# State-space projections straight from the transposed input, and the first unit's C replicas ahead of its transposes

## The chip, the cores and the metric

The kernel runs on one core of a Trainium2 chip, in fp32. The metric is the device time of one execution in microseconds; of several executions the median is given. Engines are called by name: TensorE (PE), VectorE (DVE), ScalarE (ACT), GpSimd (POOL) and SyncE (SP), whose queue issues the DMAs.

## The reference

Sixteen sequences of 512 tokens of width 128 pass attention, a mixture of eight experts, a state-space layer solved as a fixed point, and the mixture again, each with a layer norm ahead of it and a residual sum behind it. The change touches the state-space layer:

```python
xz = hidden_states @ W_in.T
x, z = (xz[..., :D_INNER], xz[..., D_INNER:])          # D_INNER = 256
x_dbl = x @ W_x.T
dt_low = x_dbl[..., :DT_RANK]                          # DT_RANK = 8
B0 = x_dbl[..., DT_RANK:DT_RANK + D_STATE]             # D_STATE = 16
C0 = x_dbl[..., DT_RANK + D_STATE:]
delta = jax.nn.softplus(dt_low @ W_dt.T + b_dt)
def fp_step(y_prev):
    x_tilde = (x - y_prev) @ W_mix.T + y_prev
    bc = _shift1(y_prev) @ W_bc.T
    Bt = bc_normalize(B0 + bc[..., :D_STATE])
    Ct = bc_normalize(C0 + bc[..., D_STATE:])
    y = _selective_scan(x_tilde, delta, A, Bt, Ct, D)  # h = exp(delta A) h + delta u B; y = sum_n h C + D u
    return layer_norm(y)
y0 = jnp.zeros_like(x)
y_star = jax.lax.fori_loop(0, 8, lambda i, y: y + STEP * (fp_step(y) - y), y0)
y = fp_step(y_star)
```

Here `hidden_states` is the layer norm of the residual; its transpose is `xnT` in the kernel. As y starts at zero, the first step needs only what comes from x.

## The kernel before, in words

A loop of 16 turns (one a sequence) runs attention, `mixture`, `ssm_inputs`, `first_unit`, an inner loop of 8 turns with two `scan_unit` each (one for each half of 256 tokens), a last `scan_unit`, `ssm_output` and `mixture`. Each engine has its own program, written out by hand in order; semaphores (the `Signal` objects) tie them together. Weights stay on the chip. The next sequence's attention start is done inside the last mixture.

`ssm_inputs` turns the normed tokens on TensorE (L444), ScalarE copies them to `xnT` (L909), then TensorE makes x transposed (`xT`, L618, 256 channels as two blocks of 128, each 512 tokens), ScalarE copies each block (L1003), TensorE makes the 8 low-rank rows (L623), ScalarE copies them to `dtlow` (L1006), whose ninth row is ones so that the bias `b_dt` rides in `w_dt`, and TensorE makes delta's argument (L628) into PSUM banks 5 and 6. B and C (L633, bank 7) and the mixed x (L639, banks 0 and 1) come from `xT` too, two matmuls for each of four token blocks, one for each block of channels.

The softplus is max(v, 0) + ln(1 + e) with e = exp(-|v|), with a correction of the rounding of 1 + e by a slope 1 - e/2. ScalarE makes Abs (L1010), Exp (L1013) and Ln (L1015); VectorE makes the max (L1439), 1 + e (L1442), the slope (L1444) and four more steps up to delta (L1459). Then ScalarE squares B and C and takes the root, VectorE multiplies x and delta (`du`, L1462) and normalises B and C into `bcn` (L1487). ACT_TABLE_LOAD rows are loads of ScalarE's function tables, which the compiler places.

A unit has 16 scans (p = 0 to 15). A scan covers a pair of channel blocks of 32 for one group m of four states. It needs da, the exponential of delta times the decay, from a replica of delta on the four state rows (`repeat_delta`, L657, block cb of eight, into banks 5, 6, 7, 4 by turns; ScalarE's exponentials, L1035, two a scan, signal `da_ready`), and its input (`scan_input`, L803, from `scan_in`, which L1470 on VectorE fills for m = 0 to 2 and L1069 on ScalarE for m = 3). In the first unit the scans follow `FIRST`: j = 0 and 1 for all four m, then the pairs j = 2, 3 for m = 2, 0, 1, 3. As both halves' da are needed, all 32 exponentials are made here. VectorE scans (L1508), and a memset at the first token of every second row (`da_cut`) cuts the state between the two rows of a scan; GpSimd multiplies each state by C (L1669), for which `crep` holds C's replicas (`first_c`, L696, bank 3, in two halves, copied at L1042), and `first_sum` adds up products on TensorE (L708) into bank 3. Scans from the fifth on wait for the product four places back and for a small DMA that keeps the last state. From p = 3 on, input p waits for scan p - 3, since three banks hold the inputs.

At the end TensorE makes the C replicas of the second half (`front_c`, L757), ScalarE fills the first inputs of the next unit (L1069 at L1157) and copies the replicas (L1159), and TensorE does the last `first_sum`. Then the loop begins with input 0 and VectorE's scans (L1569).

The order of TensorE in the first unit is: replicas 0 to 3 of delta; input 0; first half of C; input 1; replicas 4 and 5; input 2; second half of C; inputs 3 to 5; replicas 6 and 7; then inputs with sums between.

## Time and profile before

| | us |
|---|---|
| Time, median of 3 runs | 10725.11 |
| Lowest and highest of them | 10701.15, 10734.08 |
| Profiled execution, time | 10721.71 |
| Profiled execution, span | 10719.8 |
| Mean granted TensorE clock, share of full | 0.96 |

The profile is of one execution. Its page gives busy times, slices and groups of instructions for the whole span. Since every sequence runs through all stages, the timeline of one sequence (instructions in order of time, neighbours of one kind merged into one row with a count) is what shows where an engine waits; in its rows the brackets give the idle time of that engine before the row and what ended it. The clock of a stretch stands in the table of windows: 1.00 is 2.4 GHz and 0.50 is 1.2 GHz.

### The profile page before, as it was taken

The page shows a single profiled execution, that of the slowest core. Times are in us where ns is not written, and L with a number is a line of the kernel's source. Part 1 is how long each engine was busy: PE and PEld are TensorE (multiplying, and loading weights), DVE is VectorE, ACT ScalarE, POOL GpSimd, SP SyncE. Part 2 cuts the span into 40 slices and gives each one's busy share as a digit, 9 for nine tenths or more (in the row PEclk, how much of TensorE's full clock was granted, in tenths as well). Part 3 has the DMA queues.
Part 4 walks back from the last instruction along what each step waited for, and adds up shares of the span by engine and source line. Part 5 has one row for each costly group of instructions (what it writes and reads, how often), then busy time and mean ns, then how long its engine had stood idle before and what let it go on. Part 6 is the DMA issues. An engine that isn't in the chain of part 4 may idle for free.

```text
span 10719.8 us, 254606 instructions
## 1 busy us (share of the span) xinstructions
PE 9419.7 (88%) x86284; PEld 6248.4 (58%) x86284; DVE 9037.8 (84%) x16766; ACT 7334.3 (68%) x15096; POOL 6110.9 (57%) x4900
## 2 busy tenths in 40 slices
PE   7988889888898888988889888898888988889888
PEld 4656656566565665656656566565665656656566
DVE  6978879789797887978879788797887979879698
ACT  5866758677576776757768576675766857668576
POOL 1936719367293672926729277292762927639276
PEclk9999999999999999999999999999999999999999
DMA  0000000000000000000000000000000000000000
GB/s 21 0 3 1 1 3 0 3 1 1 3 0 3 1 2 3 0 3 1 2 3 0 3 1 1 3 0 3 1 1 3 0 3 1 2 2 0 3 1 3
DMA packets 648318, 23.40 MB, mean 2 GB/s; under 512 B 629169, under 2 KB 646978, under 8 KB 647362
## 3 DMA queue, kind: packets, MB, share of 16 engines
q1 hardware_dynamic: 647746, 16.11, 3.6%
q8 instruction: 318, 5.21, 0.2%
q14 instruction: 254, 2.08, 0.1%
HBM read 9.40 MB, written 4.19 MB: 1 GB/s over the span
## 4 chain that ended last, share of the span: by engine, by line
DVE 31%; PE 25%; issue 19%; POOL 17%; ACT 5%; DVEq 2%; DMA 1%; POOLq 1%; SPq 0%; ACTq 0%
POOL work L1669 16%; DVE work L1569 15%; DVE work L1559 6%; PE ps L573 4%; PE ps L578 4%; PE ps L588 3%; PE ps L521 3%; PE ps L509 2%; ACT da L947 1%; DMA hend<-work 1%; PE ps L486 1%; DVE scan_in L1470 1%; DVE stats L1187 1%; DVEq L1553 1%; PE ps L803 1%
## 5 line engine op out<-in xcount | busy, mean ns | idle before, releaser
L1669 POOL TENSOR_TENSOR work<-work,crep 128x512 f32<-128x512 f32 x4608 | 5768.7, 1278 | 4530.9 <-ACT crep L1042 3948.6
L1069 ACT ACTIVATE scan_in<-du,bcn 128x256 f32<-128x256 f32 x8832 | 3685.6, 497 | 36.9 <-PE ps L803 26.5
L1569 DVE TENSOR_TENSOR_SCAN work<-da,hend,ps 128x256 f32<-128x256 f32 x4608 | 3037.0, 724 | 31.8 <-PE ps L803 29.9
L803 PE MATMUL ps<-w_ident,scan_in 128*128 128x128 f32 x18432 | 2713.2, 282 | 278.7 <-ACT scan_in L1069 103.0
L803 PEld LDWEIGHTS ps<-w_ident,scan_in 128*128 128x128 f32 x18432 | 2032.1, 143 | 1232.8 <-issue 713.7
L1559 DVE TENSOR_TENSOR_SCAN work<-da,ps 128x512 f32<-128x512 f32 x2048 | 2363.4, 1200 | 17.0 <-PE ps L803 0.5
L793 PE MATMUL ps<-work,w_sel 128*32 128x256 f32 x17792 | 1406.2, 392 | 158.4 <-POOL work L1669 146.8
L981 ACT ACTIVATE work<-ps,w_gate_b 128x512 f32<-128x512 f32 x512 | 352.0, 687 | 895.6 <-PE ps L573 892.8
L1294 DVE TENSOR_REDUCE smax<-ps 128x1 f32<-128x512 f32 x1024 | 661.0, 686 | 202.0 <-PE ps L486 198.0
L793 PEld LDWEIGHTS ps<-work,w_sel 128*32 128x32 f32 x17792 | 355.4, 108 | 619.3 <-POOL work L1669 364.0
L947 ACT ACTIVATE da<-ps 128x512 f32<-128x512 f32 x1024 | 573.4, 596 | 164.5 <-PE ps L509 157.2
L1395 DVE SCALAR_TENSOR_TENSOR work<-ps,w_up_b,work 128x512 f32<-128x512 f32 x512 | 377.8, 749 | 272.5 <-PE ps L578 231.2
L573 PE MATMUL ps<-xnT,gate_w 128*128 128x512 f32 x1024 | 568.8, 639 | 0.0
L578 PE MATMUL ps<-xnT,up_w 128*128 128x512 f32 x1024 | 551.1, 621 | 0.0
L588 PEld LDWEIGHTS ps<-down_w,work 128*128 128x128 f32 x4096 | 489.9, 192 | 88.2 <-issue 68.9
L757 PE MATMUL ps<-w_ident,bcn 128*32 128x128 f32 x17408 | 531.0, 274 | 0.0
L1085 ACT ACTIVATE yscT<-ps 128x512 f32<-128x512 f32 x288 | 172.0, 597 | 496.0 <-PE ps L793 496.0
L588 PE MATMUL ps<-down_w,work 128*128 128x128 f32 x4096 | 501.0, 276 | 4.0 <-DVE work L1395 4.0
L1053 ACT ACTIVATE u_sb<-ps 128x512 f32<-128x512 f32 x256 | 153.3, 599 | 501.9 <-DVE du L1524 501.9
L742 PE MATMUL ps<-mix_y,yT 128*128 128x256 f32 x2048 | 489.5, 382 | 0.0
L757 PEld LDWEIGHTS ps<-w_ident,bcn 128*32 128x32 f32 x17408 | 460.0, 110 | 45.7 <-issue 43.0
L509 PE MATMUL ps<-da 98*128 98x512 bf16 x1024 | 394.9, 390 | 103.9 <-ACT da L947 59.1
(196 smaller groups left out, 12415.6 us busy)
## 6 DMA issues: line engine op xcount, KB each, us to landing
hend<-work SPq DMA_DIRECT2D x2304, 1.0 KB, 1.8
x_in<-in_x SPq DMA_DIRECT2D x17, 256.0 KB, 2.8
out<-work SPq DMA_DIRECT2D x16, 256.0 KB
gate_w<-in_gate_w SPq DMA_DIRECT2D x1, 1024.0 KB, 4.9
up_w<-in_up_w SPq DMA_DIRECT2D x1, 1024.0 KB, 7.0
down_w<-in_down_w SPq DMA_DIRECT2D x1, 1024.0 KB, 9.0
w_w_in<-in_w_in SPq DMA_DIRECT2D x1, 256.0 KB
w_w_zy<-in_w_zy SPq DMA_DIRECT2D x1, 256.0 KB
```

What stands on the lines that cost most here:

```text
L573: mm = eng.matmul(bank(u % 2), gate_w[:, e, f * P:(f + 1) * P], xnT[:], start=True, stop=True)
L578: mm = eng.matmul(bank(2 + u % 2), up_w[:, e, f * P:(f + 1) * P], xnT[:], start=True, stop=True)
L588: mm = eng.matmul(blocks(6 + e % 2)[:, tb, :], hid[:, e % 2, f, tb * P:(tb + 1) * P], down_w[:, e, f, :], start=(tb == 0 and f == 0), stop ...
L757: mm = eng.matmul(ps[GC * k:GC * (k + 1), 6 + m // 2, c:c + P], bcn[:, hf, tb, 1, n:n + 1].broadcast_to([P, GC]), ident[:], start=(m % 2 = ...
L793: mm = eng.matmul(ps[GC * q:GC * (q + 1), 3, j % 2 * TH:(j % 2 + 1) * TH], w["sel"][:], prod[:, p % PROD, q % 2 * TH:(q % 2 + 1) * TH], st ...
L803: mm = eng.transpose(ps[:, bank, c:c + P], scan_in[:, m, tb, 2 * j + s].rearrange("p k c -> p (k c)"), ident[:])
L947: eng.activation(probsT[:, h % HG, kb, :], bank(3 + (TB * h + kb) % 2), ACT.Exp, scale=SCALE).then_inc(exped.sem, exped.up(at))
L1069: ins = eng.activation(scan_in[:, m, tb, :, k, :], du[:, hf, tb, :].rearrange("p (e c) -> p e c", c=GC), ACT.Copy, scale=bcn[:, hf, tb, 0, ...
L1294: eng.tensor_reduce(smax[:, h % 2, qb:qb + 1], bank(u % 3), AX, ALU.max).then_inc(maxed.sem, maxed.up(at))
L1559: eng.tensor_tensor_scan(hst[:, p % NHID, :], da[:, 0, 2 * p:2 * p + 2, :].rearrange("p s t -> p (s t)"), bank(RING[p % 4]), 0.0, ALU.mult ...
L1569: ins = eng.tensor_tensor_scan(hst[:, p % NHID, half], da[:, 1, 2 * p + s, :], ps[:, RING[p % 4], half], hend[:, 2 * p + s:2 * p + s + 1], ...
L1669: eng.tensor_tensor(prod[:, to, :].rearrange("p (s t) -> p s t", s=2), hst[:, p % NHID, :].rearrange("p (s t) -> p s t", s=2), crep[:, hf, ...
```

## The change

Once a launch, ahead of the loop, TensorE multiplies weights with weights: the x half of `W_in` with `W_mix` (`x_mix`), with the B and C rows of `W_x` (`x_bcw`), and with the low-rank rows and then `W_dt` (`x_dt`); ScalarE copies the results out of PSUM. The factors are loaded into `work`, which is free then; `W_in`'s x half is loaded untransposed (`w_in_c`), its z half as `w_in_z`. `cT`, which lay in `dtlow`, gets a tensor of its own.

In `ssm_inputs` delta's argument, B, C and the mixed x are each made by one matmul per token block from `xnT`. `xT`, `dtlow` and their copies are gone. The bias enters by four matmuls with a contraction of one row, issued ahead of the wait for `xnT`. ScalarE does a one-column Exp between its Sqrt and the copy of `xnT`; the slope of the softplus moves from VectorE to ScalarE (Identity, signal `dl_slope`); the copy of x_mixed goes ahead of the copy of B and C and the root.

In the first unit all of C's replicas are made at once (`repeat_c`, into banks 2 and 3) between delta's replicas 1 and 2, and ScalarE copies them with one instruction ahead of its exponentials. Input 2 waits for that copy, as its bank is 2. Delta's replicas 4, 5, 6 and 7 come singly, behind inputs 3, 4, 7 and 8. VectorE's cut comes ahead of every second scan and waits for the exponentials of two scans; before, the first two cuts covered four scans each.

```diff
+FIRST_REP_AT = (3, 4, 7, 8)
...
-            "w_in": [P, 2 * DI], "w_x": [P, DB, DR + 2 * NS], "a_log": [P, NG],
-            "w_bc": [P, DB, 2 * NS], "w_zy": [P, DB, DI], "w_mix": [P, DB, DI],
+            "w_in_z": [P, DI], "a_log": [P, NG],
+            "w_bc": [P, DB, 2 * NS], "w_zy": [P, DB, DI],
...
-        w_dt = sb("w_dt", [DR + 1, DI])
+        b_dt = sb("b_dt", [1, DI])
+        x_mix = sb("x_mix", [P, DI])
+        x_bcw = sb("x_bcw", [P, 2 * NS])
+        x_dt = sb("x_dt", [P, DI])
...
+        early = {"w_mix": work[:, 0:512].rearrange("p (h d) -> p h d", h=DB),
+                 "w_x": work[:, 512:592].rearrange("p (h d) -> p h d", h=DB),
+                 "w_in_c": work[:, 592:848].rearrange("p (h d) -> p h d", h=DB),
+                 "w_dt": work[0:DR, 1024:1280]}
+        low_in = work[0:DR, 848:976]
...
             def ssm_inputs(at):
...
+                for tb in range(TB):
+                    eng.matmul(wide[:, tb, :], one[0:1, 0:1].broadcast_to([1, P]), b_dt[:],
+                               start=(tb % 2 == 0), stop=False)
                 eng.wait_ge(n_ssm.xnT.sem, n_ssm.xnT.count(at, 1))
-                for h in range(DB):
-                    mm = eng.matmul(bank(5 + h), w["w_in"][:, h * P:(h + 1) * P], xnT[:],
-                                    start=True, stop=True)
-                    mm.then_inc(xT_done.sem, xT_done.up(at))
-                for h in range(DB):
-                    eng.wait_ge(xT_copied.sem, xT_copied.count(at, h + 1))
-                    mm = eng.matmul(ps[0:DR, 4, :], w["w_x"][:, h, 0:DR], xT[:, h, :],
-                                    start=(h == 0), stop=(h == DB - 1))
-                mm.then_inc(dt_done.sem, dt_done.up(at))
-                eng.wait_ge(dt_copied.sem, dt_copied.count(at, 1))
                 for tb in range(TB):
-                    mm = eng.matmul(wide[:, tb, :], dtlow[:, tb * P:(tb + 1) * P], w_dt[:],
-                                    start=(tb % 2 == 0), stop=(tb % 2 == 1))
+                    mm = eng.matmul(wide[:, tb, :], xnT[:, tb * P:(tb + 1) * P], x_dt[:],
+                                    start=False, stop=(tb % 2 == 1))
                 mm.then_inc(dl_done.sem, dl_done.up(at))
                 for tb in range(TB):
-                    for h in range(DB):
-                        mm = eng.matmul(ps[:, 7, tb * 32:(tb + 1) * 32], xT[:, h, tb * P:(tb + 1) * P],
-                                        w["w_x"][:, h, DR:DR + 2 * NS], start=(tb == 0 and h == 0),
-                                        stop=(tb == TB - 1 and h == DB - 1))
+                    mm = eng.matmul(ps[:, 7, tb * 32:(tb + 1) * 32], xnT[:, tb * P:(tb + 1) * P],
+                                    x_bcw[:], start=(tb == 0), stop=(tb == TB - 1))
                 mm.then_inc(bc_done.sem, bc_done.up(at))
                 for tb in range(TB):
-                    for h in range(DB):
-                        mm = eng.matmul(ps[:, tb // HB, (tb % HB) * DI:(tb % HB + 1) * DI],
-                                        xT[:, h, tb * P:(tb + 1) * P], w["w_mix"][:, h, :],
-                                        start=(tb % HB == 0 and h == 0),
-                                        stop=(tb % HB == HB - 1 and h == DB - 1))
+                    mm = eng.matmul(ps[:, tb // HB, (tb % HB) * DI:(tb % HB + 1) * DI],
+                                    xnT[:, tb * P:(tb + 1) * P], x_mix[:],
+                                    start=(tb % HB == 0), stop=(tb % HB == HB - 1))
                 mm.then_inc(xmix_done.sem, xmix_done.up(at))
 
                 eng.wait_ge(x_mixed_a.sem, x_mixed_a.count(at, 1))
                 eng.wait_ge(dl_ready.sem, dl_ready.count(at, 1))
-                for cb in range(4):
-                    if cb == 2:
-                        eng.wait_ge(bc_normed.sem, bc_normed.count(at, 1))
+                for cb in range(2):
+                    repeat_delta(at, cb)
+                eng.wait_ge(bc_normed.sem, bc_normed.count(at, 1))
+                repeat_c(at, 0, 2)
+                for cb in range(2, 4):
                     repeat_delta(at, cb)
                 first_unit(at)
...
                         eng.wait_ge(scanned.sem, scanned.count(at, p - 2))
+                    elif p == 2:
+                        eng.wait_ge(c_copied.sem, c_copied.count(at, 1))
                     scan_input(at, m, j, FIRST_BANK[p])
-                    if p in (0, 2):
-                        first_c(at, p // 2)
-                    if p in (1, 5):
-                        j = 2 + p // 5
-                        eng.wait_ge(da_ready.sem, da_ready.count(at, NM * (j - 1)))
-                        repeat_delta(at, 2 * j)
-                        repeat_delta(at, 2 * j + 1)
+                    if p in FIRST_REP_AT:
+                        cb = NK + FIRST_REP_AT.index(p)
+                        eng.wait_ge(da_ready.sem, da_ready.count(at, NM * (cb // 2 - 1)))
+                        repeat_delta(at, cb)
                     if p in FIRST_SUM_AT:
                         first_sum(at, FIRST_SUM_AT.index(p))
                 front_c(at, 1, 1)
                 first_sum(at, 4)
...
+                repeat_c(at, hf, 6)
+
+            def repeat_c(at, hf, bank):
...
                             mm = eng.matmul(
-                                ps[GC * k:GC * (k + 1), 6 + m // 2, c:c + P],
+                                ps[GC * k:GC * (k + 1), bank + m // 2, c:c + P],
...
+            for h in range(DB):
+                eng.matmul(ps[:, 0, 0:DI], early["w_in_c"][:, h, :], early["w_mix"][:, h, :],
+                           start=(h == 0), stop=(h == DB - 1))
+            for h in range(DB):
+                eng.matmul(ps[:, 1, 0:2 * NS], early["w_in_c"][:, h, :], early["w_x"][:, h, DR:DR + 2 * NS],
+                           start=(h == 0), stop=(h == DB - 1))
+            for h in range(DB):
+                mm = eng.matmul(ps[0:DR, 2, 0:P], early["w_x"][:, h, 0:DR], early["w_in_c"][:, h, :],
+                                start=(h == 0), stop=(h == DB - 1))
+            mm.then_inc(folded, 1)
+            eng.wait_ge(fold_kept, 1)
+            eng.matmul(ps[:, 3, 0:DI], low_in, early["w_dt"], start=True, stop=True).then_inc(folded, 1)
+            eng.wait_ge(fold_kept, 2)
             begin_with(start, len(PE_START))
             with eng.Fori(0, B) as b:
...
             def ssm_inputs(at):
                 root(at, n_ssm)
+                eng.activation(exp_one[:], one[:], ACT.Exp)
                 copy_turned(at, n_ssm, xnT[:], bank(4))
-                for h in range(DB):
-                    eng.wait_ge(xT_done.sem, xT_done.count(at, h + 1))
-                    eng.activation(xT[:, h, :], bank(5 + h), ACT.Copy
-                        ).then_inc(xT_copied.sem, xT_copied.up(at))
-                eng.wait_ge(dt_done.sem, dt_done.count(at, 1))
-                eng.activation(dtlow[0:DR, :], ps[0:DR, 4, :], ACT.Copy
-                    ).then_inc(dt_copied.sem, dt_copied.up(at))
                 eng.wait_ge(dl_done.sem, dl_done.count(at, 1))
...
                 eng.wait_ge(dl_exp.sem, dl_exp.count(at, 1))
+                eng.activation(delta[:].rearrange("p b c -> p (b c)"), sp[1], ACT.Identity, bias=one[:], scale=-0.5
+                               ).then_inc(dl_slope.sem, dl_slope.up(at))
                 eng.activation(sp[3], sp[1], ACT.Ln, bias=one[:]).then_inc(dl_ln.sem, dl_ln.up(at))
                 eng.wait_ge(bc_done.sem, bc_done.count(at, 1))
                 eng.activation(bcq[:].rearrange("p b k n -> p (b k n)"), ps[:, 7, 0:TB * 2 * NS],
                                ACT.Square).then_inc(sq_done.sem, sq_done.up(at))
-                eng.activation(x_bc[:].rearrange("p b c -> p (b c)"), ps[:, 7, 0:P], ACT.Copy)
-                eng.wait_ge(ss_done.sem, ss_done.count(at, 1))
-                eng.activation(nrm[:], ss[:], ACT.Sqrt).then_inc(nrm_done.sem, nrm_done.up(at))
                 eng.wait_ge(xmix_done.sem, xmix_done.count(at, 1))
                 eng.activation(x_mixed[:].rearrange("p b c -> p (b c)"),
                                ps[:, 0:2, :].rearrange("p k c -> p (k c)"), ACT.Copy
                                ).then_inc(x_mixed_a.sem, x_mixed_a.up(at))
+                eng.activation(x_bc[:].rearrange("p b c -> p (b c)"), ps[:, 7, 0:P], ACT.Copy)
+                eng.wait_ge(ss_done.sem, ss_done.count(at, 1))
+                eng.activation(nrm[:], ss[:], ACT.Sqrt).then_inc(nrm_done.sem, nrm_done.up(at))
                 eng.activation(exp_one[:], one[:], ACT.Exp)
                 eng.wait_ge(du_done.sem, du_done.count(at, 1))
                 eng.wait_ge(bc_normed.sem, bc_normed.count(at, 1))
                 fill(at, 0, NM - 1, 0)
                 fill(at, 0, NM - 1, 1).then_inc(filled_a.sem, filled_a.up(at))
+                eng.wait_ge(c_rep.sem, c_rep.count(at, 1))
+                eng.activation(crep[:, 0].rearrange("p m t -> p (m t)"),
+                               ps[:, 2:4, :].rearrange("p k c -> p (k c)"), ACT.Copy
+                               ).then_inc(c_copied.sem, c_copied.up(at))
                 for p, (m, j) in enumerate(FIRST):
                     for cb in (2 * j, 2 * j + 1):
                         eng.wait_ge(dl_rep.sem, dl_rep.count(at, cb + 1))
@@ -1036,12 +1034,6 @@
                             "p (f t) -> p f t", f=2), ACT.Exp,
                                              scale=decay[:, g:g + 1])
                     ins.then_inc(da_ready.sem, da_ready.up(at))
...
+            eng.wait_ge(folded, 1)
+            eng.activation(x_mix[:], ps[:, 0, 0:DI], ACT.Copy)
+            eng.activation(x_bcw[:], ps[:, 1, 0:2 * NS], ACT.Copy)
+            eng.activation(low_in, ps[0:DR, 2, 0:P], ACT.Copy).then_inc(fold_kept, 1)
+            eng.wait_ge(folded, 2)
+            eng.activation(x_dt[:], ps[:, 3, 0:DI], ACT.Copy).then_inc(fold_kept, 1)
...
-                eng.tensor_scalar(sp[2], sp[1], 1.0, None, ALU.add)
+                eng.tensor_scalar(sp[2], sp[1], 1.0, None, ALU.add).then_inc(vchain.sem, vchain.up(at))
                 flat = delta[:].rearrange("p b c -> p (b c)")
-                eng.tensor_scalar(flat, sp[1], -0.5, 1.0, ALU.mult, ALU.add
-                                  ).then_inc(vchain.sem, vchain.up(at))
                 eng.wait_ge(vchain.sem, vchain.last(at))
                 eng.scalar_tensor_tensor(out=sp[2], in0=sp[2], scalar=-1.0, in1=sp[1],
                                          op0=ALU.add, op1=ALU.subtract
                                              ).then_inc(vchain.sem, vchain.up(at))
                 eng.wait_ge(vchain.sem, vchain.last(at))
+                eng.wait_ge(dl_slope.sem, dl_slope.count(at, 1))
                 eng.tensor_tensor(sp[2], sp[2], flat, ALU.mult).then_inc(vchain.sem, vchain.up(at))
...
-                    if p in (0, 4):
-                        eng.wait_ge(da_ready.sem, da_ready.count(at, p + 4))
-                        eng.memset(da[:, 0, g + 1::NCB, 0], 0.0).then_inc(da_cut.sem, da_cut.up(at))
-                        eng.wait_ge(da_cut.sem, da_cut.last(at))
-                    if p >= 8 and p % 2 == 0:
+                    if p % 2 == 0:
                         eng.wait_ge(da_ready.sem, da_ready.count(at, p + 2))
-                        eng.memset(da[:, 0, g + 1:g + 4:2, 0], 0.0).then_inc(da_cut.sem, da_cut.up(at))
+                        step = NCB if p < NP // 2 else 2
+                        eng.memset(da[:, 0, g + 1:g + step + 2:step, 0], 0.0).then_inc(da_cut.sem, da_cut.up(at))
                         eng.wait_ge(da_cut.sem, da_cut.last(at))
```

Left out of the diff: the semaphores of removed and added steps, the loads' count, the memset of `dtlow` and the arrays' preparation on the host.

## Rows read from the trace of the kernel before

**Rows 1.** Page, part 1: busy us of each engine (share of span), xinstructions.
```profile
PE 9419.7 (88%) x86284; PEld 6248.4 (58%) x86284; DVE 9037.8 (84%) x16766; ACT 7334.3 (68%) x15096; POOL 6110.9 (57%) x4900
```

**Rows 2.** Timeline of VectorE in the loop: start, length, engine, line, operation.
```profile
248.60 0.18 DVE L1516 TENSOR_REDUCE ss<-bcq 128x4 f32<-128x64 f32 x1
...
295.25 0.19 DVE L1516 TENSOR_REDUCE ss<-bcq 128x4 f32<-128x64 f32 x1
```

**Rows 3.** Timeline, all engines, 177 to 188 us: projections of the first sequence.
```profile
177.33 1.10 PE L444 MATMUL ps<-w_ident,work 128*128 128x128 f32 x4 [3.47 <-DVE work L1205]
...
178.47 0.60 ACT L909 ACTIVATE xnT<-ps 128x512 f32<-128x512 f32 x1 [1.78 <-PE ps L444]
...
179.12 3.62 PE L618 MATMUL ps<-xnT,w_w_in 128*128 128x512 f32 x4 [0.69 <-ACT xnT L909]
...
185.22 1.99 PE L628 MATMUL ps<-w_dt,dtlow 9*128 9x256 f32 x8 [0.68 <-ACT dtlow L1006]
...
187.25 1.02 ACT L1010 ACTIVATE scan_in<-ps 128x1024 f32<-128x1024 f32 x1 [2.08 <-PE ps L628]
```

**Rows 4.** Timeline, 188 to 198 us: softplus of the first sequence.
```profile
188.29 1.28 ACT L1013 ACT_TABLE_LOAD   x1
...
188.31 1.23 DVE L1439 TENSOR_SCALAR scan_in<-ps 128x1024 f32<-128x1024 f32 x1 [9.19 <-ACT scan_in L1010]
...
189.59 1.06 ACT L1013 ACTIVATE scan_in<-scan_in 128x1024 f32<-128x1024 f32 x1
...
191.28 0.69 DVE L1444 TENSOR_SCALAR delta<-scan_in 128x1024 f32<-128x1024 f32 x1
...
196.08 1.22 DVE L1459 TENSOR_TENSOR delta<-scan_in 128x1024 f32<-128x1024 f32 x1
```

**Rows 5.** Timeline, 199 to 215 us: fills, exponentials, replicas, first product.
```profile
199.33 6.90 DVE L1470 TENSOR_TENSOR scan_in<-du,bcn 128x1024 f32<-128x1024 f32 x6
...
199.39 3.31 ACT L1069 ACTIVATE scan_in<-du,bcn 128x256 f32<-128x256 f32 x8 [0.55 <-DVE bcn L1487]
...
202.60 4.69 ACT L1035 ACTIVATE da<-ps,decay 128x512 f32<-128x512 f32 x8
...
207.34 3.64 PE L657 MATMUL ps<-w_ident,delta 128*32 128x128 f32 x64 [2.68 <-ACT da L1035]
...
207.55 2.33 DVE L1508 TENSOR_TENSOR_SCAN work<-da,ps 128x512 f32<-128x512 f32 x2
...
213.68 0.60 ACT L1042 ACTIVATE crep<-ps 128x512 f32<-128x512 f32 x1 [3.58 <-PE ps L696]
...
214.36 19.78 POOL L1669 TENSOR_TENSOR work<-work,crep 128x512 f32<-128x512 f32 x16 [213.91 <-ACT crep L1042]
```

**Rows 6.** Timeline, 221 to 234 us: end of the first unit, loop's first scan.
```profile
221.86 2.33 DVE L1508 TENSOR_TENSOR_SCAN work<-da,ps 128x512 f32<-128x512 f32 x2 [0.29 <-PE ps L803]
...
227.96 3.30 ACT L1069 ACTIVATE scan_in<-du,bcn 128x256 f32<-128x256 f32 x8 [1.66 <-PE ps L803]
...
229.70 1.93 PE L757 MATMUL ps<-w_ident,bcn 128*32 128x128 f32 x64
...
232.30 1.09 PE L803 MATMUL ps<-w_ident,scan_in 128*128 128x128 f32 x8
...
233.25 5.21 DVE L1569 TENSOR_TENSOR_SCAN work<-da,hend,ps 128x256 f32<-128x256 f32 x8 [1.27 <-PE ps L803]
```

**Rows 7.** Windows: length, busy (count) of PE, PEld, DVE, ACT, POOL; clock; DMA; GB/s.
```profile
178.00:180.00 2.00, 1.31 (x3) 0.64 (x3) 0.96 (x2) 0.60 (x1) 0.00 (x0) 0.76 0.00 0
...
180.00:182.00 2.00, 2.00 (x4) 0.67 (x2) 0.00 (x0) 0.60 (x1) 0.00 (x0) 0.50 0.00 0
...
182.00:184.00 2.00, 2.00 (x6) 0.27 (x4) 0.00 (x0) 0.60 (x1) 0.00 (x0) 0.89 0.00 0
...
208.00:210.00 2.00, 2.00 (x44) 1.85 (x40) 1.89 (x2) 2.00 (x4) 0.00 (x0) 0.50 0.00 0
...
228.00:230.00 2.00, 0.76 (x20) 0.59 (x24) 1.77 (x4) 2.00 (x6) 2.00 (x2) 1.00 0.15 1
```

51 lines of the change are left out of this document (14 added, 37 removed).

## The prediction, made before the change was run

> **What bounds the kernel now.** I read the page's busy times first. TensorE is busy 88% of the span and VectorE 84% [rows 1], but such a share is a mean over stages, so it prices nothing. The order of time comes next. In the fixed-point loop the first `ss` reduction of two neighbouring turns stands at 248.60 and 295.25 us [rows 2], so a turn takes 46.65 us, and in the whole launch there are 16 sequences of 8 turns. The change leaves the turns alone. It works on the stretch ahead of them: from the normalised transposes of the state-space input (177.33) to the first scan of the loop (233.25) [rows 3, 6]. That stretch is a chain with waits and little overlap, so time taken off it should come off every sequence. It runs 16 times; in the tenth and the sixteenth sequence it is as long within 0.2 us, in the fifth 1.3 us shorter.
>
> I cut the stretch at three moments: *a*, the start of the Abs on ScalarE, 187.25 [rows 3]; *D*, the end of the last addition into delta, 196.08 + 1.22 = 197.30 [rows 4]; and *L*, the first scan of the loop, 233.25 [rows 6]. So D is a + 10.05 and L is D + 35.95.
>
> **Part 1: projections, transposes to a.** Removed: the 128x512 matmuls of L618 (3.62 us), two ScalarE copies of xT, the L623 matmuls, and the dtlow copy between them and L628 [rows 3]; every hop was PE to ACT and back. Added: four one-row bias matmuls (each of this kernel's fp32 matmuls has two records, so 8 records of 256 columns), issued behind the transposes and ahead of the wait for xnT; then 8 records of the same width from xnT. The nearest rows are the 8 records of L628, 1.99 us at full clock, 0.25 each [rows 3]; its contraction has 9 rows, no row shows one of 1, and I take the same price, since L618 and L628 share columns and not rows and both follow the columns. At half clock I take 0.43 a record (L618: 3.62/4 = 0.91 for twice the columns, mostly at half clock). The clock matters: TensorE sits idle 3.47 us before these transposes, its clock is 0.76 of full in 178 to 180, 0.50 in 180 to 182 and 0.89 in 182 to 184 [rows 3, 7], which puts the low stretch at about 179.1 to 182.5. I assume that it stays there. The transposes end at 178.43. To 179.1 some 2.8 bias records pass; the other 5.2 cost 2.24, to 181.35. To 182.5 pass 2.7 of the xnT records, the other 5.3 at 0.23 end at 183.7. So a = 183.75, 3.5 us earlier. If the clock stays low for all of them: 178.43 + 0.7 + 13.2 x 0.43 = 184.8, or 185.2 with drains, and the gain is 2.05. If the bias rows cost less, a is near 183.4 and the gain 3.85.
>
> The xnT copy (178.47 to 179.07) must not be late. Ahead of it ScalarE now does a table load and the one-column Exp. It idles 1.78 us before that copy, from 176.69 [rows 3]; 1.28 for the load [rows 4] and 0.2 fit, and even 1 us of lateness would be covered by the bias matmuls, which run to 181.35. I cost it at nothing; without both covers it would be 1.5.
>
> **Part 2: softplus, a to D.** Now Abs (1.02), table load 188.29 (1.28), Exp (1.06), and then VectorE until D [rows 3, 4]. The load goes away, because the table came earlier: 1.28 us. No row shows Abs or Identity right behind an Exp; Abs runs here behind a Sqrt table and the loop's Identity runs behind one too. The Trainium skill (ScalarE: Activation LUTs, "Table sets: the hidden batching unit") says copy, identity and abs are in every set; no run here shows it for these two. The same page ("What ACT_TABLE_LOAD costs") prices a switch at 1.28 for the load and 1.38 more for a drain; this trace shows the load 0.02 us behind the Abs [rows 3, 4] and nothing like a drain, and by the page the sum below would gain 1.38 x 16 = 22 us more. The slope (L1444, 0.69 long, next instruction 0.72 later by the rows) [rows 4] moves to ScalarE, an Identity of 1.06 like the Exp, which finishes under the 1.23 us of the two-operand step. VectorE starts the add about 0.6 earlier relative to the rest. Against it: the max L1439 (1.23) lay under the table load and now ends at a + 2.29, 0.19 after the Exp [rows 4]. So D = a + 10.05 - 1.28 - 0.6 + 0.19 = a + 8.35, gain 1.7; Ln, still 1.28 load and 1.15 long but behind the Identity, ends at a + 5.65, ahead of the final addition (a + 7.1). Square, x_mixed (1.01), x_bc, Sqrt load and nrm now end at a + 8.8, and VectorE asks for nrm after du, at about D + 1.3 = a + 9.6: hidden by 0.8. x_mixed needs its matmuls, now 8 records instead of 16 and ending by a + 4.5 even at half clock, against a + 5.95. Bounds of this part: 1.4 (each hop 0.1 worse) to 1.9 (the max hidden).
> Together D moves from 197.30 to 192.1, gain 5.2, between 3.45 and 5.75.
>
> **Part 3: first unit, D to L.** Today VectorE starts the first scan at D + 10.25, only when four exponential pairs are there (eight records from 202.60, 0.586 each); TensorE issues half of the C replicas behind the second pair of delta replicas, ScalarE copies them at 213.68 after a 3.58 us wait, and GpSimd starts at 214.36 = D + 17.06, running 16 products in 19.78 [rows 5]. Since a scan from the fifth on waits for a product, this start paces all.
> New order on TensorE: delta replicas 0 and 1, wait for bcn (D + 2.0), all C replicas (64 records, 1.93 us as in L757 [rows 6]), replicas 2 and 3. TensorE has by then been idle for 5 us (mix ends near 186.5), and idling 3.47 us was enough for a low clock soon after [rows 3, 7], so I charge half clock to the first pair: 3.64, as L657 at 207.34 [rows 5] against the 1.93 of L757 for as many records at full clock [rows 6]. It ends at D + 3.75, C at 5.7. ScalarE's own fill ends at D + 5.4 [rows 5], then the C copy of 1.02 to D + 6.8. The wait placed ahead of the exponentials costs them 202.60 -> D + 5.3 against D + 6.8: 1.5 us later, repaid because two copies and the 3.58 wait are gone. First pair of exponentials 9.1; VectorE's fills end at 8.93 [rows 5]; first scan D + 9.3 (now only two pairs awaited, each pair of scans behind one memset). GpSimd starts at D + 10.5, 6.6 earlier. TensorE's new wait for the C copy before input 2 holds back inputs 2 to 15, and is over at D + 6.8; input 2 also needs VectorE's fill at 8.93, so it costs nothing.
> Then VectorE at 2.58 a pair (2.33 for the two scans at 221.86, 0.25 for memset and waits) [rows 6]: fifth scan over at 15.65. Input 7 waits for it: 16.35, replica 6 17.3, input 8 18.0, replica 7 18.95 (0.66 an input, half of 1.93 a replica). ScalarE has done nine pairs at 17.35, waits for replica 7, and ends pair 10 at 19.55; six more at 1.17 end at 26.6. VectorE wants that pair at 19.6, so the stall hardly touches it. Input 15 at 27.25, ScalarE's fill of the next unit 3.30 [rows 6], 30.6; loop input to first scan 0.95 [rows 6]; L = D + 31.6. GpSimd's 14th product, for which the last partial sum waits and which holds L now, is done at 28.5. Gain 35.95 - 31.6 = 4.35. GpSimd is free for the loop at D + 33.7 against 39.25, so it doesn't take the place. Bounds: 1.9 if a second low stretch covers inputs 3 to 8 (about 2.4: two replicas and two inputs at half speed and one replica more), 5.0 if none occurs and replica 7 comes earlier.
>
> **Once per launch.** One more weight load, six matmuls, three copies, a matmul and a copy stand ahead of the first normalisation. I estimate some 16 records, most of half the width of L618's or less, at 3.0 in all from that line's price, and the load and the chained copies at 1.5 from L909's 0.60 a copy of 512 columns [rows 3]: 4.5 us, between 3 and 7. Nothing covers it.
>
> **Sum.** 16 x (5.2 + 4.35) = 153; less 4.5, and less 4 for a sequence or two in which the low clock falls worse: 144. The profiled execution took 10721.71, 1.9 over its span and 3.4 under the median 10725.11. 10721.7 - 144 + 3.4 = 10581 us.
>
> **Rivals.** (1) *The clock takes back the second gain.* With fewer matmuls and over 5 us of idleness, TensorE is at half clock from D until replica 7. C replicas end at D + 7.6, the copy at 8.65, first scan 11.2, replica 7 23.4, L = D + 36.5, gain -0.5; with a at 185.2 also, 3.2 a sequence, 51 in all: 10678. For it: 208 to 210 are at 0.50 today although TensorE is busy throughout [rows 7]. Against: the low stretch seen in 178 to 184 was over by 182.5, with TensorE at work [rows 7]. The Trainium skill (TensorE: Matmul & The Clock Gate, Part 1) says that the throttled state is the default and activity releases it, which speaks against removing matmuls; by that rule the time is this rival's. Chance 0.12.
> (2) *Table loads stay.* If Abs or Identity doesn't live in the Exp table, one or two loads of 1.28 return: 16 x 2.56 = 41, 10622. Chance 0.06.
> (3) *Slower.* Half clock lasts to the loop. Then inputs (1.12) and partial sums (1.28) pace the end too: input 15 at D + 35, C of the next unit 3.9, last sum 41.5, L = D + 43, 7 later than now against a first gain of 3.75: 3.3 lost, 53 + 4.5, 10782. It decides for slower from where the low stretch outlasts about input 12. Against it: in 228 to 230 TensorE works 0.76 us of 2 and is at full clock [rows 7]. Chance 0.05.
> (4) *More*, under 10545: bias rows cheap and no second low stretch. Chance 0.07. The forecast itself 0.70.
>
> **How the numbers follow.** The bounds of the parts give 16 x (3.45 + 1.9) - 7 = 79 to 16 x (5.75 + 5.0) - 3 = 169, so 10646 to 10556 by the median; rival 2 lies inside, and 10 us below is room for the terms that I rounded. Range 10545 to 10645, which leaves out rivals 1, 3 and 4, about 0.22. About 0.3% (32 us) is what a measurement can tell from no change. Faster by more: 0.91; within: 0.04, the tails of rivals 1 and 3; slower: 0.05.
>
> **What would show it.** Right: Abs starting 5.3 us after the xnT copy instead of 8.8, no table load between Abs and Exp, delta done 8.35 after Abs; one 1.02 us C copy before the exponentials; GpSimd's first product some 10.5 us after D, first scan of the loop 31.6 after. Wrong: the clock at 0.50 in several 2 us stretches behind D, replica 7 holding ScalarE longer than 2 us, or a loop turn other than 46.65, which would make all of this small beside 128 times the difference.

## The result and the profile after

The changed kernel took 10604.16 us (median of 4 runs, 10599.98 to 10630.49) against 10721.96 for the kernel before on the same chip: a ratio of 0.9897, with a 95% interval of 0.988 to 0.9914, so some 110 us less by the ratio (92 to 129), 118 by the two medians. The same kernel timed twice more beside the experiments gave 0.9885 (0.9868 to 0.9901) and 0.9916 (0.9903 to 0.993). The forecast was 10581 in a range of 10545 to 10645. Its profiled execution took 10630.49 (span 10628.6), 91 under that of the kernel before, and was the slowest of its four.

Page of the changed kernel, part 1: busy us of each engine (share of span), xinstructions.

```profile
PE 9367.1 (88%) x86042; PEld 6259.7 (59%) x86042; DVE 9021.3 (85%) x16781; ACT 7321.0 (69%) x15068; POOL 6111.1 (57%) x4900
```

Beside [rows 1] nothing moves by more than 0.6%. The stretch that the change works on has to be read in the order of time. Timeline of the changed kernel, first sequence, from the turned norm to the end of delta: start, length, engine, line, operation, records, and in brackets the idle time ahead and what ended it.

```profile
181.65 1.10 PE L450 MATMUL ps<-w_ident,work 128*128 128x128 f32 x4 [3.47 <-DVE work L1203]
...
182.68 3.15 PE L623 MATMUL ps<-b_dt,one 1*128 1x256 f32 x8
182.78 0.60 ACT L907 ACTIVATE xnT<-ps 128x512 f32<-128x512 f32 x1 [0.27 <-PE ps L450]
...
185.76 3.78 PE L627 MATMUL ps<-x_dt,xnT 128*128 128x256 f32 x8
...
189.58 1.02 ACT L1002 ACTIVATE scan_in<-ps 128x1024 f32<-128x1024 f32 x1 [6.20 <-PE ps L627]
...
190.64 1.06 ACT L1005 ACTIVATE scan_in<-scan_in 128x1024 f32<-128x1024 f32 x1
...
191.73 1.15 ACT L1007 ACTIVATE delta<-scan_in,one 128x1024 f32<-128x1024 f32 x1
...
192.90 1.28 ACT L1009 ACT_TABLE_LOAD   x1
...
194.19 1.15 ACT L1009 ACTIVATE scan_in<-scan_in,one 128x1024 f32<-128x1024 f32 x1
...
196.57 1.22 DVE L1456 TENSOR_TENSOR delta<-scan_in 128x1024 f32<-128x1024 f32 x1
```

The Abs starts 6.80 us after the xnT copy (forecast 5.3, before 8.78 in [rows 3]), and delta is done at 197.79, 8.21 after the Abs (forecast 8.35). No table load stands between Abs, Exp and Identity. The bias records take 3.15 and the xnT records 3.78, where 8 records of this width took 1.99 at full clock in [rows 3]. The windows say why. Windows of the changed kernel: length, busy (count) of PE, PEld, DVE, ACT, POOL, granted clock, DMA share, GB/s.

```profile
182.00:184.00 2.00, 2.00 (x8) 1.40 (x9) 1.27 (x3) 1.10 (x3) 0.00 (x0) 0.84 0.00 0
184.00:186.00 2.00, 2.00 (x6) 1.16 (x5) 0.00 (x0) 0.00 (x0) 0.00 (x0) 0.50 0.00 0
186.00:188.00 2.00, 2.00 (x5) 1.61 (x6) 0.00 (x0) 0.00 (x0) 0.00 (x0) 0.50 0.00 0
188.00:190.00 2.00, 2.00 (x8) 1.67 (x7) 0.00 (x0) 0.42 (x1) 0.00 (x0) 0.50 0.00 0
190.00:192.00 2.00, 2.00 (x13) 1.84 (x13) 1.36 (x2) 1.94 (x3) 0.00 (x0) 0.96 0.00 0
...
200.00:202.00 2.00, 2.00 (x46) 2.00 (x42) 2.00 (x2) 2.00 (x6) 0.00 (x0) 0.50 0.01 4
```

In [rows 7] the low stretch covered about 179.1 to 182.5; here half clock holds for three whole windows, while TensorE is busy throughout, and it holds all but the first two or three of the 16 records (0.84 in 182 to 184 puts its start at about 183.4, 0.96 in 190 to 192 its end at about 190.2). From delta to the loop, same timeline:

```profile
197.93 3.64 PE L654 MATMUL ps<-w_ident,delta 128*32 128x128 f32 x64 [5.41 <-DVE delta L1456]
...
201.32 3.16 PE L742 MATMUL ps<-w_ident,bcn 128*32 128x128 f32 x64
...
204.29 1.93 PE L654 MATMUL ps<-w_ident,delta 128*32 128x128 f32 x64
204.55 1.02 ACT L1026 ACTIVATE crep<-ps 128x1024 f32<-128x1024 f32 x1 [1.46 <-PE ps L742]
...
208.14 2.33 DVE L1502 TENSOR_TENSOR_SCAN work<-da,ps 128x512 f32<-128x512 f32 x2
...
209.61 6.22 POOL L1662 TENSOR_TENSOR work<-work,crep 128x512 f32<-128x512 f32 x5 [209.16 <-DVE work L1502]
...
210.25 1.60 PE L654 MATMUL ps<-w_ident,delta 128*32 128x128 f32 x32 [0.17 <-ACT da L1033]
...
212.82 1.66 PE L654 MATMUL ps<-w_ident,delta 128*32 128x128 f32 x32
...
217.02 0.69 ACT L1033 ACTIVATE da<-ps,decay 128x512 f32<-128x512 f32 x1 [1.05 <-PE ps L654]
...
218.62 7.62 ACT L1033 ACTIVATE da<-ps,decay 128x512 f32<-128x512 f32 x13 [0.91 <-PE ps L654]
...
230.54 1.09 PE L788 MATMUL ps<-w_ident,scan_in 128*128 128x128 f32 x8 [0.78 <-ACT scan_in L1061]
...
231.49 5.21 DVE L1563 TENSOR_TENSOR_SCAN work<-da,hend,ps 128x256 f32<-128x256 f32 x8 [1.65 <-POOL work L1662]
...
246.32 0.18 DVE L1510 TENSOR_REDUCE ss<-bcq 128x4 f32<-128x64 f32 x1
...
292.82 0.19 DVE L1510 TENSOR_REDUCE ss<-bcq 128x4 f32<-128x64 f32 x1
```

GpSimd no longer waits for the C copy [rows 5] but for the first scan, and starts 11.8 us after delta instead of 17.06. The C replicas ran mostly at half clock too (3.16). ScalarE waits 1.05 and 0.91 for replicas 6 and 7, and the loop's first scan comes 33.70 after delta. Its bracket names GpSimd, but its input starts 0.95 ahead of it, as in the kernel before (232.30 and 233.25, [rows 6]), and that input waits for ScalarE's fill.

Half clock comes back once more behind delta. Windows of the same execution:

```profile
210.00:212.00 2.00, 1.83 (x34) 1.37 (x34) 1.86 (x4) 2.00 (x5) 2.00 (x2) 0.66 0.15 1
212.00:214.00 2.00, 2.00 (x28) 1.59 (x31) 1.70 (x3) 2.00 (x4) 2.00 (x3) 0.50 0.07 1
```

This second stretch, from about 210.6 to 214.0, falls on replicas 4 and 5, which take 1.60 and 1.66 instead of 1.08, and on an input. It is there in 13 of the 16 sequences, whose first scan of the loop comes 33.44 to 33.73 after delta. In the other three (the tenth, thirteenth and sixteenth) half clock ends by 3.0 us after delta, the C replicas take 1.94, the second stretch comes only some 27 us after delta, and the loop's first scan comes at 32.36.

The first turn of the loop is 46.50 us here. The median turn is 46.53 in the kernel before and 46.52 in this one, so the 46.65 of [rows 2] was a turn slightly longer than most.

Means over all 16 sequences of each profiled execution, read from the same rows. The first column runs from the start of the xnT copy to the Abs, then to *D*, then to *L*; the fourth is their sum; the last is the timed ratio to the kernel before on the same chip.

| kernel | copy to a | a to D | D to L | copy to L | ratio (95%) |
|---|---|---|---|---|---|
| before | 8.81 | 10.05 | 35.46 | 54.33 | 1 |
| changed | 6.95 | 8.21 | 33.38 | 48.54 | 0.9897 (0.988-0.9914) |
| e1 changed again | 6.89 | 8.21 | 33.23 | 48.33 | 0.9885 (0.9868-0.9901) |
| e2 projections, softplus only | 6.86 | 8.21 | 33.95 | 49.02 | 0.9911 (0.9894-0.9927) |
| e3 first unit only | 8.82 | 10.04 | 32.24 | 51.10 | 0.995 (0.9934-0.9967) |
| e4 without the softplus part | 6.99 | 10.05 | 32.02 | 49.06 | 0.9893 (0.9877-0.991) |
| e5 TensorE busy ahead of D | 6.93 | 8.21 | 33.58 | 48.72 | 0.9929 (0.9912-0.9945) |
| e6 bias rows early | 4.35 | 8.21 | 33.25 | 45.81 | 0.9876 (0.986-0.9893) |
| e7 replicas earlier | 7.06 | 8.21 | 32.69 | 47.96 | 0.9915 (0.9899-0.9932) |
| e8 e5, e6 and e7 | 4.34 | 8.21 | 31.59 | 44.14 | 0.9859 (0.9842-0.9875) |
| e9 changed, on a third chip | 6.99 | 8.21 | 33.29 | 48.49 | 0.9916 (0.9903-0.993) |
| e10 bias on 128 rows | 5.20 | 8.21 | 32.07 | 45.48 | 0.9875 (0.986-0.989) |
| e11 TensorE busy ahead of the transposes | 6.74 | 8.21 | 33.00 | 47.95 | 0.9911 (0.9896-0.9926) |
| e12 e10, early, with e5 and e7 | 4.20 | 8.21 | 31.66 | 44.07 | 0.9861 (0.9846-0.9876) |

The stretch lost 5.79 us a sequence, 93 a launch, less 4.3 for the work ahead of the first sequence: 88 of the 91 us between the two profiled executions. What remains of a sequence beside this stretch lasted 613.1 us before and 612.9 after, but 613.2 and 610.5 in the two further profiles of the changed kernel itself (e1, e9): some 42 us a launch between two executions of one program, outside this stretch. It goes with the clock: in that part of a sequence TensorE is at half clock for 36.3 us in e1 and 33.9 in e9, and over the sequences of all fourteen profiles the length of the part and its time at half clock have a correlation of 0.72. Why the clock differs between two executions no run here explains. The table's stages are therefore the finer instrument, and times are compared by the medians and intervals of one chip alone. Even the ratio of one kernel moves between chips: 0.9885 (e1) and 0.9916 (e9) have intervals that do not meet. The changed kernel was not timed on the chip of e5 to e8, so their ratios are set against a base that is uncertain by 0.3%.

### The profile page after: what moved, and what is told of

Same layout as the page of the kernel before. It is cut to its first block, busy times and chain, and to the rows that moved or that the text cites. A ratio compares the mean times of both kernels' runs of the same rounds, so it can differ in the third digit from the quotient of the medians.

```text
span 10628.6 us, 254158 instructions
## 1 busy us (share of the span) xinstructions
PE 9367.1 (88%) x86042; PEld 6259.7 (59%) x86042; DVE 9021.3 (85%) x16781; ACT 7321.0 (69%) x15068; POOL 6111.1 (57%) x4900
## 3 DMA queue, kind: packets, MB, share of 16 engines
q14 instruction: 254, 2.08, 0.1%
## 4 chain that ended last, share of the span: by engine, by line
DVE 31%; PE 27%; issue 17%; POOL 15%; ACT 5%; DVEq 2%; DMA 1%; POOLq 1%; SPq 0%; ACTq 0%
DVE work L1563 15%; POOL work L1662 15%; DVE work L1553 6%; PE ps L579 4%; PE ps L584 4%; PE ps L594 3%; PE ps L527 2%; PE ps L515 2%; PE ps L788 1%; ACT da L945 1%; DMA hend<-work 1%; PE ps L492 1%; PE ps L654 1%; DVE stats L1185 1%; DVEq L1547 1%
## 5 line engine op out<-in xcount | busy, mean ns | idle before, releaser
L742 PE MATMUL ps<-w_ident,bcn 128*32 128x128 f32 x18432 | 579.8, 279 | 0.0
L742 PEld LDWEIGHTS ps<-w_ident,bcn 128*32 128x32 f32 x18432 | 507.3, 112 | 47.0 <-issue 44.3
```

What stands on the lines that cost most here:

```text
L742: mm = eng.matmul(ps[GC * k:GC * (k + 1), bank + m // 2, c:c + P], bcn[:, hf, tb, 1, n:n + 1].broadcast_to([P, GC]), ident[:], start=(m % ...
```

## The experiments

**e1, the changed kernel again**, as the base for e2, e3 and e4 on their chip.

> The changed kernel once more, for its clock and stage lengths beside the partial kernels. Both theories: 0.989 of before; copy of xnT to the loop's first scan 48.5 us as a mean of the 16 sequences, against 54.3. If the profiled execution of the first result was an unlucky one (it took 10630 where three others took 10600 to 10608), this one should show fewer or shorter stretches at half clock: some 1 us less in the stages a (Abs) and L (first scan of the loop).

It measured 10604.16, and its stages repeat those of the changed kernel within 0.2 us.

**e2, projections and softplus alone**: the changed kernel with the first unit's old order.

```diff
-                for cb in range(2):
-                    repeat_delta(at, cb)
-                eng.wait_ge(bc_normed.sem, bc_normed.count(at, 1))
-                repeat_c(at, 0, 2)
-                for cb in range(2, 4):
+                for cb in range(4):
+                    if cb == 2:
+                        eng.wait_ge(bc_normed.sem, bc_normed.count(at, 1))
                     repeat_delta(at, cb)
...
+                    if p in (0, 2):
+                        first_c(at, p // 2)
```

> Weight products, bias rows, table ahead and slope on ScalarE, but the old order of the first unit (C replicas in two halves behind inputs 0 and 2, delta replicas in pairs). Theory A (each part is worth what its stage shows in the changed kernel): the stages up to D give 1.86 + 1.84 = 3.7 us a sequence, D to L stays 35.5: 16 x 3.7 - 4.3 = 55 us, ratio 0.9949. Theory B (the projections' shortcut takes from the first unit by making TensorE idle, so that its replicas run at half clock): D to L gets longer than 35.5, ratio above 0.997 if by 2 us.

It measured 10627.55, 100 us less than before; D to L is 33.95, 1.5 less than before, though this part of the program is the old one. Timeline of e2, first sequence:

```profile
207.31 1.95 PE L653 MATMUL ps<-w_ident,delta 128*32 128x128 f32 x64 [1.24 <-ACT da L1040]
...
210.93 0.60 ACT L1047 ACTIVATE crep<-ps 128x512 f32<-128x512 f32 x1 [0.87 <-PE ps L692]
...
211.60 18.52 POOL L1678 TENSOR_TENSOR work<-work,crep 128x512 f32<-128x512 f32 x15 [211.15 <-ACT crep L1047]
```

The replicas that took 3.64 in [rows 5] take 1.95, and the wait of 3.58 ahead of the second C copy is 0.87. With delta some 3.8 us sooner after the copy, the low stretch falls on other instructions. The gain of this part is larger than the stages up to delta say.

**e3, first unit alone**: the kernel before with the new order of replicas, one C copy and a memset for each second scan.

```diff
-                for cb in range(4):
-                    if cb == 2:
-                        eng.wait_ge(bc_normed.sem, bc_normed.count(at, 1))
+                for cb in range(2):
+                    repeat_delta(at, cb)
+                eng.wait_ge(bc_normed.sem, bc_normed.count(at, 1))
+                repeat_c(at, 0, 2)
+                for cb in range(2, 4):
                     repeat_delta(at, cb)
...
-                    if p in (0, 2):
-                        first_c(at, p // 2)
```

> The kernel before with only the new order of the first unit. Theory A: D to L falls from 35.5 to 33.4, 2.1 x 16 = 33 us, ratio 0.997. Theory B: with the old projections TensorE is warm at D, C replicas take 1.93 instead of 3.2 and the first pair of delta replicas 1.93 instead of 3.6; D to L falls to 32 or less, 3.5 x 16 = 56 us, ratio 0.995.

It measured 10669.39, 58 us less. Timeline and a window of e3, first sequence:

```profile
196.84 1.96 PE L659 MATMUL ps<-w_ident,delta 128*32 128x128 f32 x64 [3.10 <-ACT x_mixed L1013]
198.74 1.95 PE L747 MATMUL ps<-w_ident,bcn 128*32 128x128 f32 x64
```

```profile
198.00:200.00 2.00, 2.00 (x79) 1.78 (x72) 1.90 (x6) 1.44 (x6) 0.00 (x0) 1.00 0.05 12
```

Behind the old projections the same replicas run at full clock, and D to L is 32.24, 1.1 shorter than in the changed kernel. The two halves alone give 100 and 58 us, together 123 (e1). By the stages, copy to L, they give 5.31 and 3.23 a sequence and together 6.00, not 8.54. The parts don't add.

**e4, without the softplus part**: no early Exp, slope back on VectorE.

```diff
-                eng.activation(exp_one[:], one[:], ACT.Exp)
...
-                eng.activation(delta[:].rearrange("p b c -> p (b c)"), sp[1], ACT.Identity, bias=one[:], scale=-0.5
-                               ).then_inc(dl_slope.sem, dl_slope.up(at))
...
+                eng.tensor_scalar(flat, sp[1], -0.5, 1.0, ALU.mult, ALU.add
+                                  ).then_inc(vchain.sem, vchain.up(at))
```

> The changed kernel without the early Exp table and with the slope back on VectorE. If this part is worth what its stage shows, a to D returns from 8.21 to 10.05 and the time is 1.84 x 16 = 29 us over the changed kernel, ratio 0.992. Rival: the gain is hidden, because a later step (root, fills, C copy) ends last anyway: then it stays at 0.989.

It measured 10611.86, 8 us over e1 and not 29; 8 us is within the intervals of the two. The stage a to D is 1.84 longer, as it should be, but D to L is 1.21 shorter, so copy to L is 0.73 longer, some 12 us a launch. TensorE's first C replicas take 2.14 us instead of 3.16: coming 1.84 us later to D, they meet less of the low stretch. And in none of the 16 sequences does half clock come back before the loop. The step's own size was right, its worth was not.

**e5, TensorE kept busy until D.** Five idle matmuls behind the projections write into bank 3, which the C replicas overwrite before anything reads it.

```diff
                 mm.then_inc(xmix_done.sem, xmix_done.up(at))
+                for _ in range(5):
+                    eng.matmul(bank(3), ident[:], xnT[:], start=True, stop=True)
```

> The changed kernel with five idle 512-column matmuls (into PSUM bank 3, read by nobody) behind the mixed-x matmuls, so that TensorE works through the wait for delta; nothing that is used is changed. Clock theory: delta replicas 0 and 1 and the C replicas fall from 3.64 and 3.16 to about 1.93 each, D to L from 33.3 to about 32, as in the kernel with only the new order (32.24): 1.2 x 16 = 19 us less than the changed kernel, ratio 0.987. Rival: the replicas aren't what D to L hangs on (fills and exponentials are): 0.9885 as the changed kernel, D to L at 33.3.

The first replicas take 1.96, the C replicas 1.95, and the first scan comes 9.00 after D instead of 10.02 in the mean; yet the time is not better (10631.98, 0.9929), and D to L is 33.58 in the mean. In all 16 sequences half clock came back twice before the loop, some 9 and 26 us after D, and in 8 of them each of the two stretches was twice as long as in the others. Windows and timeline of e5, third sequence:

```profile
1528.00:1530.00 2.00, 2.00 (x33) 1.55 (x33) 1.87 (x4) 2.00 (x4) 2.00 (x2) 0.50 0.15 1
...
1546.00:1548.00 2.00, 2.00 (x26) 1.17 (x29) 1.77 (x4) 1.56 (x4) 0.98 (x2) 0.50 0.18 9
```

```profile
1552.06 1.38 DVE L1565 TENSOR_TENSOR_SCAN work<-da,hend,ps 128x256 f32<-128x256 f32 x2 [3.30 <-PE ps L790]
```

The second stretch falls on the last inputs, the partial sums and the next C replicas, and VectorE waits 3.30 us for the loop's first input. Those 8 sequences have a D to L of some 34.9, the others some 32.3. The low stretch was moved, not removed: between the copy and L TensorE is at half clock for 17.2 us in the mean, against 16.6 in the changed kernel.

**e6, the bias rows ahead of the transposes**, behind a wait for the addition that last reads their banks.

```diff
-                turn_norm(at, n_ssm, blocks(4))
+                eng.wait_ge(summed.sem, summed.count(at, NE - 1))
                 for tb in range(TB):
                     eng.matmul(wide[:, tb, :], one[0:1, 0:1].broadcast_to([1, P]), b_dt[:],
                                start=(tb % 2 == 0), stop=False)
+                turn_norm(at, n_ssm, blocks(4))
```

> The changed kernel with the four bias matmuls ahead of the transposes instead of behind them, in the 3.47 us in which TensorE waits for the normalised tokens. Clock theory: the xnT matmuls find a TensorE that has worked shortly before and take 2 us, so Abs starts 2.7 us after the copy of xnT instead of 6.8: 4.1 us a sequence less, of which a part returns behind D; between 20 and 65 us under the changed kernel, ratio 0.983 to 0.987. Rival (the clock falls all the same): xnT matmuls 3.4 us long, Abs at 4.2, and everything given back behind D: ratio 0.988.

It measured 10579.72, 0.9876; its interval still overlaps e1's. Timeline of e6, first sequence:

```profile
179.19 1.99 PE L623 MATMUL ps<-b_dt,one 1*128 1x256 f32 x8
...
183.86 0.60 ACT L908 ACTIVATE xnT<-ps 128x512 f32<-128x512 f32 x1 [0.26 <-PE ps L450]
...
184.51 3.58 PE L628 MATMUL ps<-x_dt,xnT 128*128 128x256 f32 x8 [0.69 <-ACT xnT L908]
```

At full clock the one-row records cost what the forecast took: 1.99 for eight. The price was right, the clock wasn't. The xnT records behind still meet half clock, so the Abs comes 4.35 after the copy, as the rival said. Its other half, that all of this comes back behind D, is not in the stages: D to L is 33.25, as in e1.

**e7, replicas 4 to 7 earlier**: they ride on inputs 3, 4, 5 and 6, and ScalarE's fill for the next unit waits for 12 inputs instead of 16.

```diff
-FIRST_REP_AT = (3, 4, 7, 8)
+FIRST_REP_AT = (3, 4, 5, 6)
...
-                eng.wait_ge(b_done.sem, b_done.count(at, NP))
+                eng.wait_ge(b_done.sem, b_done.count(at, 12))
```

> The changed kernel with delta replicas 6 and 7 behind inputs 5 and 6 instead of 7 and 8, and with ScalarE's fill of the next unit's first inputs waiting for 12 inputs of this unit instead of 16. If ScalarE's wait for replicas 6 and 7 (1.05 + 0.91 us) and its 0.81 us wait for input 15 set the loop's first scan: 1.7 to 2.5 us less from D to L, 27 to 40 us, ratio 0.985. Rival: GpSimd's products end last, first scan only 0.7 us earlier, 11 us, ratio 0.9875.

D to L is 32.69, 0.6 less, as the rival had it; as a time (10620.53, 0.9915) that is inconclusive.

**e8, e5, e6 and e7 together.**

> The edits of the three kernels beside it together. If they add up: copy of xnT to the loop's first scan 48.4 - 4.1 - 1.2 - 2 = 41 us, 117 us under the changed kernel, ratio 0.9775. If the half clock gives part back again, as it did between the parts of the change: ratio 0.981 to 0.985.

It measured 10561.09, 0.9859, less of a gain than either expectation: copy to L is 44.14, 4.4 less than in the changed kernel and not 7.3. The edits of e5 and e7, of little worth alone, bring 1.7 beside e6. Here low stretches did go away: between the copy and L TensorE is at half clock for 6.9 us in the mean instead of 16.6, and in 8 of 16 sequences it has full clock from D to L. What remains of a sequence is longest here, 613.7.

**e9, the changed kernel in the third group.**

> The changed kernel as the base for the three kernels beside it, on their chip: ratio 0.9885 again, Abs 6.9 us after the copy of xnT, clock at half from about 183 to 190 us in the first sequence.

It measured 10606.13, with the stages of e1, but a ratio of 0.9916 and not 0.9885.

**e10, the bias on 128 rows.** The bias is loaded on all partitions and multiplied by the identity: the same 8 records of 256 columns in the same place, with 128 rows of contraction instead of one. The stationary operand changes with the rows, from one element read 128 times to the identity.

```diff
-        b_dt = sb("b_dt", [1, DI])
+        b_dt = sb("b_dt", [P, DI])
...
-                    eng.matmul(wide[:, tb, :], one[0:1, 0:1].broadcast_to([1, P]), b_dt[:],
+                    eng.matmul(wide[:, tb, :], ident[:], b_dt[:],
```

> The changed kernel with its four bias matmuls contracted over 128 rows (the identity times the bias on 128 partitions, the same sum) instead of one; columns, records and order are as they were. Theory R (rows count for the clock: one-row matmuls look like an idle TensorE): the half clock that sets in behind the transposes ends after 3.4 us as in the kernel before, during the xnT matmuls; Abs 5.3 us after the copy instead of 6.9, 1.6 x 16 = 25 us less if nothing is given back, ratio 0.986. Theory C (only columns and busy time count): no difference, Abs at 6.9, 0.9885.

It measured 10563.24, 43 us under e9 on the same chip. Timeline of e10, sixth sequence, and its windows:

```profile
3468.26 2.88 PE L623 MATMUL ps<-b_dt,w_ident 128*128 128x256 f32 x8
3468.46 0.60 ACT L907 ACTIVATE xnT<-ps 128x512 f32<-128x512 f32 x1 [0.27 <-PE ps L450]
...
3470.93 2.63 PE L627 MATMUL ps<-x_dt,xnT 128*128 128x256 f32 x8
...
3473.60 1.02 ACT L1002 ACTIVATE scan_in<-ps 128x1024 f32<-128x1024 f32 x1 [4.54 <-PE ps L627]
```

```profile
3468.00:3470.00 2.00, 2.00 (x8) 1.65 (x8) 0.95 (x2) 0.79 (x2) 0.00 (x0) 0.75 0.00 0
3470.00:3472.00 2.00, 2.00 (x6) 1.56 (x5) 0.00 (x0) 0.00 (x0) 0.00 (x0) 0.50 0.00 0
3472.00:3474.00 2.00, 2.00 (x13) 1.78 (x12) 0.00 (x0) 0.40 (x1) 0.00 (x0) 0.89 0.00 0
```

Half clock fills one window instead of three, and the Abs starts 5.14 after the copy here and 5.20 in the mean: the forecast's 5.3. That D to L also becomes 32.07, close to the forecast's 31.6, was a surprise: the next stretch came sooner too and ended 4.2 us after D instead of 6.0, so the C replicas take 2.28 instead of 3.16, and in 15 of 16 sequences half clock doesn't come back before the loop. From the first scan to L it is 22.6 in those, against 23.35 in the changed kernel's 13 sequences with the stretch on replicas 4 and 5.

**e11, TensorE busy ahead of the transposes**: three idle matmuls into bank 1, which the projections overwrite.

```diff
+                for _ in range(3):
+                    eng.matmul(bank(1), ident[:], xnT[:], start=True, stop=True)
                 turn_norm(at, n_ssm, blocks(4))
```

> The changed kernel with three idle 128-row, 512-column matmuls ahead of the transposes, in the 3.47 us in which TensorE waits for the tokens (PSUM bank 1, read by nobody). If the idle time before the transposes is what sets the half clock off: no low stretch at 183, bias rows 2 us and xnT matmuls 2 us, Abs 4 us after the copy, up to 45 us less, ratio 0.985. Rival: the one-row bias matmuls bring the low clock themselves, one stretch later: low from about 186 on, Abs at 5, ratio 0.9875.

It measured 10605.23, e9's time, and the Abs comes 6.74 after the copy, so neither expectation held. Timeline and windows of e11, first sequence:

```profile
178.77 2.74 PE L622 MATMUL ps<-xnT,w_ident 128*128 128x512 f32 x6
...
182.41 1.10 PE L450 MATMUL ps<-w_ident,work 128*128 128x128 f32 x4 [0.89 <-DVE work L1205]
...
183.44 3.20 PE L625 MATMUL ps<-b_dt,one 1*128 1x256 f32 x8
```

```profile
182.00:184.00 2.00, 1.59 (x7) 1.06 (x8) 1.83 (x5) 1.72 (x3) 0.00 (x0) 1.00 0.00 0
184.00:186.00 2.00, 2.00 (x6) 1.54 (x5) 0.19 (x1) 0.14 (x1) 0.00 (x0) 0.52 0.00 0
```

TensorE idles 0.89 us instead of 3.47 ahead of the transposes and is at full clock for them, and the clock falls inside the one-row records, with the engine 2.00 of 2.00 busy. So cutting the idle time to 0.89 us was not enough to hold the clock. What brings it down there was not isolated: it falls 0.3 to 1.0 us after the start of the copy in most sequences of the kernel before, of e10 and of e12 too, which have no one-row records.

**e12, the best of these together**: one idle matmul and the 128-row bias ahead of the transposes, with e5 and e7.

```diff
+                for _ in range(1):
+                    eng.matmul(bank(1), ident[:], xnT[:], start=True, stop=True)
+                eng.wait_ge(summed.sem, summed.count(at, NE - 1))
+                for tb in range(TB):
+                    eng.matmul(wide[:, tb, :], ident[:], b_dt[:],
+                               start=(tb % 2 == 0), stop=False)
                 turn_norm(at, n_ssm, blocks(4))
-                for tb in range(TB):
-                    eng.matmul(wide[:, tb, :], one[0:1, 0:1].broadcast_to([1, P]), b_dt[:],
-                               start=(tb % 2 == 0), stop=False)
```

> All of it: one idle matmul and the 128-row bias matmuls ahead of the transposes, five idle matmuls through the wait for delta, replicas 6 and 7 of delta behind inputs 5 and 6, and the next unit's fill waiting for 12 inputs. Clock theory: Abs 2.7 to 3 us after the copy, D to L 31.2 to 32.1 as in the kernel with the last three edits, copy to the loop's first scan 42.5 against 48.3: 16 x 5.8 = 93 us under the changed kernel, ratio 0.980. Rival (what is gained comes back as a low stretch elsewhere in the sequence, as with the idle matmuls alone): 0.985 or more.

It measured 10550.96, 0.9861 (0.9846 to 0.9876): 147 us less than the kernel before and 55 less than e9, as the rival had it and not the 93 expected. Copy to L is 44.07 and not 42.5: in 15 of 16 sequences the clock falls behind the copy all the same, and the Abs comes at 4.20 in the mean; in the first, where it doesn't, the Abs comes at 2.68. It is the shortest time here, with e8's ratio (0.9859) beside it, and its lead over e10 (12 us) is within what the rest of a sequence varies by.

## Why the prediction was right, and where its steps were not

The direction and the range held; the size was 110 us (92 to 129) against 144. By the stages the forecast's 9.55 us a sequence became 5.79. Point by point:

**Part 1, the step that failed.** It took for the one-row bias records "the same price, since L618 and L628 share columns and not rows and both follow the columns", and for the low stretch: "I assume that it stays there." The first half held (1.99 in e6). The second did not: half clock lasted from about 183.4 to 190.2, 6.8 us, where the prediction had kept the 3.4 us of the kernel before. The gain was 1.86 instead of 3.5, just under the lower bound of 2.05, which had been worked out for just this case of a low clock for all records. It was under it because a record at half clock cost 0.47 (3.78 for eight) and not the 0.43 taken from L618, which ran partly at full clock. e10 shows the cause: with the columns, the records and their order kept and the rows changed from 1 to 128 (and the stationary operand with them), half clock begins at the same place but lasts 3.4 us less, the Abs comes 5.20 after the copy, and the launch is 43 us shorter. With one row TensorE is busy 2.00 of 2.00 in three windows at 0.50 and its clock doesn't rise. The Trainium skill (TensorE: Matmul & The Clock Gate, Part 1) says that the throttled state is the default and activity releases it; by that rule alone the two kernels should not differ, if activity is what the profile shows as busy, and they do, by 1.79 us a sequence (e9, e10). Bias matmuls of other heights weren't tried.

**The clock rival.** Its mechanism was there, and half of its place. It put the Abs at 185.2 where the forecast had 183.75; less the 4.3 us of the longer start the Abs came at 185.3. Behind D it expected half clock without a break to replica 7. There were two stretches instead, until 6.0 us after D and from 12.9 to 16.3: the first replicas and most of the C replicas, then replicas 4 and 5; between them the second pair, at 204.29, takes 1.93 again, and replicas 6 and 7 take 1.08. The gain of 5.79 a sequence lies between its 3.2 and the forecast's 9.55, somewhat nearer to its own.

**Part 2, right.** 1.84 instead of 1.7, no load between Abs, Exp and Identity, and the Ln runs 0.01 after its load ends (192.90 + 1.28). The Trainium skill (ScalarE: Activation LUTs, "Table sets: the hidden batching unit") agrees with the first; the drain of 1.38 us that "What ACT_TABLE_LOAD costs" adds is not to be seen, and the 22 us more that it would have given didn't come. In the whole, though, the part is worth 0.73 us a sequence and not 1.84 (e4), because the sooner D comes, the more of the low stretch the replicas meet.

**Part 3, right in its mechanism, too large in three terms.** The gain was 2.08, not 4.35. The baseline of 35.95 was the first sequence's; the mean is 35.46, as 5 of 16 sequences have 34.4: 0.5 gone by pricing from one sequence, though the prediction had seen the shorter fifth. In those five, half clock behind D ends at 12.6 instead of 15.9. The C replicas were priced at 1.93 and took 3.16 at half clock, so the exponentials start at D + 7.68 instead of 6.8. Replica 7 was put at D + 18.95 and ends near D + 20.8: a single replica of 32 records takes 1.08 at full clock, not half of 1.93, the scans that the inputs wait for are later by then, and the second low stretch, which the prediction had only in its lower bound, costs another 0.75 (from the first scan to L 23.35, and 22.6 in e10 without it); the last exponential ends at D + 28.45 instead of 26.6, and L at D + 33.7 instead of 31.6. GpSimd starts at D + 11.49 in the mean instead of 10.5. The bounds of 1.9 to 5.0 hold it. The prediction charged half clock to the first pair alone, because two stages were summed as if the clock in one didn't depend on the other; e3 (same replicas, full clock), e4 and e10 show that it does. Where the clock is nearly as it assumed, its sum is nearly right: D to L is 32.07 in e10.

**Once per launch, right.** The first xnT copy moved from 178.47 to 182.78: 4.31 against 4.5. In e1 and e9 it is 4.1 and 6.0, inside the bounds of 3 to 7.

**The turn, harmless.** 46.65 was one turn's length and not, as the prediction has it, every turn's. The mean over all turns is 46.75 before and 46.71 after, and 46.79 and 46.58 in e1 and e9, so the change left the turns alone.

**Size and luck.** The stages account for 88 to 92 us in the three profiled executions of this kernel; the three timed comparisons give some 90 to 123. The difference lies in the rest of the sequence, and that the time came within 23 us of the forecast is in part luck: by the stages alone the gain was 88 of 144, and the time would have been some 10637, near the end of the range.

**Open.** In most sequences of the changed kernel, copy to L is 48.7 although the Abs varies by 0.3. The traces show a balance: in the eleventh sequence the low stretch begins 0.28 sooner than in the first and the Abs comes 0.27 later, but the next stretch ends 0.28 sooner too, and the C replicas end 21.7 us after the copy in both. Not found was what makes the clock fall behind the copy at all, which of rows and stationary operand counts in e10, and why the rest of a sequence differs by 2.7 us between two executions of one kernel.

## What to carry to other kernels

A matmul that adds a bias by one row of contraction is dear where the clock is low: here it filled TensorE and didn't bring the clock up. Spread the bias over all rows (e10) or issue it where the clock is full (e6). Whenever matmuls are removed or an engine's wait is shortened, ask which later instructions the low stretch will then fall on; price each stage with the clock at both levels, and try the parts together, since gains of 100 and 58 made 123 here. Take the baseline of a repeated stretch as the mean over all its repeats, not from the first.

## What the runs showed of the hardware

- Eight records of 256 columns contracting one row took 1.99 us at full clock (e6). Where the clock was low, TensorE stayed at 0.50 for 6.8 us with them and 3.4 with 128 rows in their place: the Abs at 6.99 us after the copy against 5.20 (e9, e10).
- The clock can fall while TensorE is busy without a gap in the profile: 0.52 in 184 to 186 us of e11, inside one-row records, 1.65 us after an idle time of 0.89 had ended.
- Keeping TensorE busy through one wait moved the low stretches: first replicas from 3.64 to 1.96 us in e5, 3.30 us of waiting at the end of the unit in 8 of 16 sequences, and 17.2 us at half clock between the copy and L against 16.6. Together with the bias ahead of the transposes and earlier replicas (e8) it left 6.9.
- 64 replica records took 1.93 us at full and 3.64 at half clock; 32 alone took 1.08 at full.
